# ScalarE's rounding of the next item's scores and of the weights change places in step 6 of a one-core attention kernel

## The chip, the cores and the metric

The kernel runs on one core of a Trainium2 chip (trn2). The metric is the device time of one execution in microseconds (us). Engines are named as the profile names them: PE (TensorE), ACT (ScalarE), DVE (VectorE), POOL (GpSimd), SP (the queue that issues most of the DMAs).

## What is computed

An audio tower: a token mixer (an attention over a spectrum, a feed-forward part, a second attention whose output sets the weights of a moving window), a retention layer, and then a product-key attention layer, which takes most of the time:

```python
q = (x @ Wq).reshape(b, n, HEADS, DIM) * DIM ** (-0.5)
kv_scores, indices = _pk(x, Wq_pk, pk_keys)        # top 16 of 64 x 64 key pairs, softmax over them
k = jnp.einsum('bnhk,bnhkd->bnhd', kv_scores, keys_table[ind])
v = jnp.einsum('bnhk,bnhkd->bnhd', kv_scores, values_table[ind])
sim = jnp.einsum('bihd,bjhd->bhij', q, k)          # causal
out = jnp.einsum('bhij,bjhd->bhid', softmax(sim), v)
```

There are 8 heads, 8 sequences of 344 tokens, and tables of 4096 rows of 64 values and 64 keys for each head.

## The kernel before, in words

Nothing is gathered. For each pair of head and sequence (an item; 64 in all, in the order of the heads) the kernel makes the weight of every one of the 4096 table rows for each of the 344 tokens, zero for all rows but the 16 chosen, and multiplies the table by them on PE. The table has 32 chunks of 128 rows, and an item takes 16 steps (`d` from 0 to 15) of two chunks each:

- **Logarithms of the weights.** `log_weights` (line 981): two fp16 matmuls of a 0/1 matrix `sel` with `X`, 128x344 each, into one of two pairs of PSUM banks (`d % 2`).
- **Weights.** ACT takes the exponential, `exponentials` (line 1218), into `W` in a ring of eight. DVE sets to zero what is below the threshold, `weights` (line 1575), and with that also sets free the PSUM banks.
- **Sum over the table.** `table_sum` on PE. Even steps: fp32 matmuls (line 990). Odd steps (`SPLITS`): `W` is split in a rounded part and the rest, `weights_high` on ACT (line 1223) and `weights_low` on POOL (line 1409), and four matmuls of line 998 and two of line 1002 take the place of the two.

PE runs ahead with the logarithms: in step `d` it first waits for `weights` of `d + 3` (`w_done`), then makes the logarithms of `d + 5`, then the table sum of `d`. ACT in step `d` takes the exponential of `d + 5` and rounds the weights of `d + 3`. Where `d + 5` reaches 16 these belong to the next item. So from step 11 on PE needs the next item's `X`.

`X` of the next item comes by this chain. DVE finds the largest scores; POOL subtracts the thresholds and clamps (`centre_first`, `clamp_scores`, lines 1351, 1356 and 1358, in step 4) into `aS`. In step 6 ACT rounds `aS` to fp16, `high_part` (line 1213, writes `spl`); POOL makes the remainder, `low_part` (line 1403); SP then issues six transposing DMAs from `spl` to `X` (`turn_scores`, line 860), three for the even part and three for the odd part, one behind the other. PE waits for the even part ahead of its step 11 (`x_even`) and for the odd part in step 15 (`x_odd`).

Every engine's order is written out by hand in a loop body, one for each engine. What touches the change:

```python
def high_part(n):
    act.wait_ge(clamped, n * 2 + 2)
    ...
    A(spl[:, :, :, 0, :], aS[:, :, :, :], ACT.Copy).then_inc(high_ready, 1)
```

Step 6 of the other engines: POOL has `low_part` and then `weights_low` of step 9, and in front of them, from step 4, `clamp_scores` and `weights_low` of step 7; in step 7 it goes on with `chosen_weights` (line 1395). DVE has `weights` of step 10, then (in items of even number, `par == 0`) `copy_second_queries`, then `chosen` (line 1615: three small comparisons), then `weights` of step 11. In items of even number ACT has `copy_queries` (line 1243) behind the exponential of step 6. In step 11 PE's table sum is followed by `turn_probabilities` (line 1076), in step 13 by `attention_output` (line 1084), in step 7 by `attention_scores`.

Of the kernel before, what the change touches and what calls it, by code (L numbers as in the profile page):

```python
# [663 lines left out]
def retention_and_keys(nc, ps, hT, x2T, epst, cst, const, weight, wf, sel, eyeb, causb, wq, wo, tables, out):  # L664
# [14 lines left out]
    with ExitStack() as ctx:  # L679
# [96 lines left out]
        def ahead(s):  # L776
            return AHEAD[s]
# [52 lines left out]
        with nc.Block() as block:  # L830
# [335 lines left out]
            def _(act):  # L1166
# [28 lines left out]
                def copy_similarities(n):  # L1195
                    act.wait_ge(sim_mm, n + 1)
                    if not isinstance(n, int) or n > 0:
                        act.wait_ge(a_ready, n * 2)
                    A(sS[:, 0:2, :, :], ps[:, sim_bank(n), 0:256], ACT.Copy)
                    A(sS[0:88, 2, :, :], ps[0:88, sim_bank(n), 256:384], ACT.Copy).then_inc(sim_ready, 1)  # L1200

                def candidate_weights(n):
                    act.wait_ge(rel_ready, n + 1)
                    A(ecs[:, :, :], ecs[:, :, :], ACT.Exp)
                    act.wait_ge(thr_step, n * 2 + 2)
                    A(small[:, EDT, :], small[:, DT, :], ACT.Exp).then_inc(ecs_ready, 1)

                def high_part(n):
                    act.wait_ge(clamped, n * 2 + 2)
                    if not isinstance(n, int):  # L1210
                        act.wait_ge(x_even, n * 48)
                        act.wait_ge(x_odd, n * 48)
                    A(spl[:, :, :, 0, :], aS[:, :, :, :], ACT.Copy).then_inc(high_ready, 1)  # L1213

                def exponentials(i, d):
                    act.wait_ge(main_done, i * NDC + (d - RING + 1 + ahead(main_done)))
                    act.wait_ge(log_mm, i * NDC + (d + 1))
                    A(W[:, d % RING, :, :], ps[:, 2 * (d % 2):2 * (d % 2) + 2, 0:LOUT], ACT.Exp).then_inc(e_done, 1)  # L1218

                def weights_high(i, d):  # L1220
                    act.wait_ge(main_done, i * NDC + (split_before(d, SPLIT_RING) + 1 + ahead(main_done)))
                    act.wait_ge(w_done, i * NDC + (d + 1))
                    A(W_high[:, split_at(d) % SPLIT_RING, :, :], W[:, d % RING, :, :], ACT.Copy).then_inc(high_done, 1)  # L1223

                def table_high(slot, loads, pair, half):

                    act.wait_ge(s_tab[slot], loads * 48)
                    o, rows = part_of(tab_high, slot, pair, half), rows_of(slot, pair, half)
                    A(o, rows, ACT.Copy).then_inc(tab_high_ready, 1)

                def copy_gains(i):
                    act.wait_ge(gains_mm, i + 1)
                    A(gains[:, :], ps[:, MID1, 0:LOUT], ACT.Copy).then_inc(gains_ready, 1)

                def copy_projected_values(i):
                    act.wait_ge(vw_mm, i + 1)
                    act.wait_ge(nmax_done, i * 3 + 3)
                    A(vw[:, 0:2, :], ps[:, MID0, NT * 128:NT * 128 + 128], ACT.Copy)
                    A(vw[0:88, 2, :], ps[0:88, MID1, LOUT:LOUT + 64], ACT.Copy).then_inc(vw_ready, 1)

                def copy_queries(g):
                    act.wait_ge(q_mm, g + (1 + ahead(q_mm)))
                    A(qT[64:128, 0, :], ps[64:128, 5, 0:LOUT], ACT.Copy, scale=D ** -0.5).then_inc(qT_ready, 1)

                def probabilities(i, pj, t):
                    act.wait_ge(nmax_done, i * 3 + 3)
                    m, (bank, c0) = TT[t][1], score_area(t, pj)
                    A(P[0:m, t, 0:TT[t][0] + m], ps[0:m, bank, c0:c0 + TT[t][0] + m], ACT.Exp, bias=nmax[0:m, t:t + 1],  # L1248
                      accum_out=zz[0:m, t:t + 1]).then_inc(p_done, 1)

                def copy_turned_probabilities(i):
                    act.wait_ge(pt_mm, i + 1)
                    A(PT[:, 0, :], ps[:, MID1, 0:LOUT], ACT.Copy)
                    A(PT[0:88, 2, 0:88], ps[0:88, MID1, LOUT:LOUT + 88], ACT.Copy).then_inc(pt_ready, 1)  # L1254
# [31 lines left out]
                class Body:  # L1286
# [4 lines left out]
                    @staticmethod  # L1291
                    def item(i, slot, par, g, pair):
                        nj = 1 - par
                        for d in range(NDC):
                            if d + LEAD < NDC:
                                exponentials(i, d + LEAD)
                            else:
                                exponentials(i + 1, d + LEAD - NDC)
                            if d == 6 and par == 0:
                                copy_queries(g)  # L1300
                            if (d + LEAD - 2) % NDC in SPLITS:
                                if d + LEAD - 2 < NDC:
                                    weights_high(i, d + LEAD - 2)
                                else:
                                    weights_high(i + 1, d + LEAD - 2 - NDC)
                            if d == 2:
                                copy_gains(i)
                            if d == 5:
                                candidate_weights(i + 1)
                            if d == 6:  # L1310
                                high_part(i + 1)
                            if d == 8:
                                copy_similarities(i + 2)
                            if d == 9:
                                copy_projected_values(i)
                                for t in range(NT):
                                    probabilities(i, nj, t)
                            if d == 12:
                                copy_turned_probabilities(i)
                            if d == 11:  # L1320
                                table_high(1 - slot, i // 16 + (1 + slot), pair, par)
# [481 lines left out]
```

## Time and profile before

| | before |
|---|---|
| median of 3 runs | 1924.92 us (1922.6 to 1926.18) |
| profiled execution, its own time | 1926.57 us |
| its span, first to last instruction | 1924.8 us |
| granted PE clock, mean | 0.987 of full |
| PE busy | 1867.0 us (97%) |
| PE weight loads busy | 1408.0 us (73%) |
| DVE busy | 1608.8 us (84%) |
| ACT busy | 1459.5 us (76%) |
| POOL busy | 1317.6 us (68%) |

The span holds some 220 us of token mixer, retention and set-up, and then the 64 items. Times in the rows are microseconds from the start of the span. An item from 962.1 to 988.5 us has an even number and one from 988.5 to 1014.3 us an odd one; these two stand for all the others. In a timeline a row gives the start, the time taken, the engine, line, operation and names, with a count where rows are merged, and in brackets the idle time ahead of it and what ended it. Rows of PE are matmuls, rows of PEld the weight loads that run ahead of them; `k_` is the prefix of this stage's tiles.

### The profile page before, as it was taken

To read this page: it belongs to the slowest core of one execution; us is meant where nothing else is said; L and a number is where in the kernel's file an instruction comes from. 1 tells how busy PE (TensorE), PEld (TensorE's weight loads), DVE (VectorE), ACT (ScalarE), POOL (GpSimd) and SP (SyncE) were. 2 spreads that over 40 slices of the span, in tenths; PEclk is the share of its full clock that TensorE was granted. 3 is DMA by queue.
4 is the path that set the end of the run, shared out by engine and by line. 5 is a ranking of instruction groups with operands and counts; after the bars stand their busy time and mean duration, and the time that the engine had idled before them with its cause. 6 is when DMAs were issued, how large, how long until landed. Compare 5 with 4: busy or idle time off the path is not lost.

```text
span 1924.8 us, 43767 instructions
## 1 busy us (share of the span) xinstructions
PE 1867.0 (97%) x11488; PEld 1408.0 (73%) x11488; DVE 1608.8 (84%) x4825; ACT 1459.5 (76%) x2969; POOL 1317.6 (68%) x1576
## 2 busy tenths in 40 slices
PE   7997899999999999999999999999999999999997
PEld 5765577777777777777777777777777777777775
DVE  4646788888888888888888888888988888888886
ACT  3853488877878777888887778887887787878885
POOL 1112377777777777777777777777777777777775
PEclk8998899999999999999999999999999999999998
DMA  3001110001000200011000200020001100020001
GB/s 110 2 1 48 58 22 21 21 16 61 20 21 21 63 17 17 21 52 33 21 16 17 63 21 21 21 61 17 19 21 32 54 16 17 18 65 21 21 19 28
DMA packets 118622, 58.00 MB, mean 30 GB/s; under 512 B 110224, under 2 KB 116560, under 8 KB 117261
## 3 DMA queue, kind: packets, MB, share of 16 engines
q1 hardware_dynamic: 115778, 56.75, 11.4%
q10 hardware_dynamic: 2795, 0.70, 0.2%
q8 instruction: 18, 0.29, 0.1%
q14 instruction: 31, 0.25, 0.0%
HBM read 24.55 MB, written 0.70 MB: 13 GB/s over the span
## 4 chain that ended last, share of the span: by engine, by line
POOL 42%; issue 38%; PE 7%; POOLq 2%; DVE 1%; SPq 0%; ACT 0%; DMA 0%; DVEq 0%; ACTq 0%
POOL k_W_low L1409 25%; POOL k_aS L1351 3%; POOL k_cand L1365 2%; POOL k_ecs L1395 2%; POOL k_tab_low L1414 2%; PE ps L990 2%; POOL k_aS L1358 2%; PE ps L981 1%; PE ps L998 1%; POOL k_aS L1356 1%; POOLq L1408 1%; POOL k_small L1380 1%; POOL k_small L1381 1%; POOL k_ecs L1376 1%; POOL k_off L1385 1%
## 5 line engine op out<-in xcount | busy, mean ns | idle before, releaser
L1409 POOL TENSOR_TENSOR k_W_low<-k_W,k_W_high 128x688 fp32r<-128x688 f32 x513 | 851.2, 1659 | 320.9 <-ACT k_W_high L1223 317.6
L1218 ACT ACTIVATE k_W<-ps 128x688 f32<-128x688 f32 x1029 | 770.0, 748 | 339.6 <-PE ps L981 327.2
L1575 DVE SCALAR_TENSOR_TENSOR k_W<-ps,k_W 128x688 f32<-128x688 f32 x1028 | 887.9, 866 | 162.9 <-ACT k_W L1218 152.6
L990 PE MATMUL ps<-k_W,k_tab 128*128 128x344 f32 x2048 | 676.4, 453 | 0.0
L981 PE MATMUL ps<-k_X,sel 128*128 128x344 f16 x2058 | 472.4, 311 | 17.1 <-DMA k_X<-k_spl 9.0
L990 PEld LDWEIGHTS ps<-k_W,k_tab 128*128 128x128 f32 x2048 | 366.2, 190 | 126.9 <-issue 0.2
L1223 ACT ACTIVATE k_W_high<-k_W 128x688 fp32r<-128x688 f32 x513 | 398.0, 776 | 0.8
L998 PE MATMUL ps<-k_W_high,k_tab_high 128*128 128x344 f32 x1024 | 386.2, 380 | 0.0
L981 PEld LDWEIGHTS ps<-k_X,sel 128*128 128x128 f16 x2058 | 164.6, 98 | 237.6 <-issue 77.1
L998 PE MATMUL ps<-k_W_high,k_tab_low 128*128 128x344 f32 x1024 | 323.9, 319 | 0.0
L1002 PE MATMUL ps<-k_W_low,k_tab_high 128*128 128x344 f32 x1024 | 246.6, 322 | 0.0
L998 PEld LDWEIGHTS ps<-k_W_high,k_tab_high 128*128 128x128 f32 x1024 | 193.7, 189 | 24.7
L998 PEld LDWEIGHTS ps<-k_W_high,k_tab_low 128*128 128x128 f32 x1024 | 193.9, 189 | 0.0
L1002 PEld LDWEIGHTS ps<-k_W_low,k_tab_high 128*128 128x128 f32 x1024 | 174.7, 188 | 3.0
L1403 POOL TENSOR_TENSOR k_spl<-k_aS,k_spl 128x480 f16<-128x480 f32 x65 | 72.9, 1122 | 56.5 <-ACT k_spl L1213 56.5
L1615 DVE TENSOR_SCALAR k_rc<-k_cand,k_small 128x100 f32<-128x100 f32 x195 | 102.5, 579 | 0.0
L1035 PE MATMUL ps<-k_kv,k_qT 64*128 64x128 f32 (+2 forms) x390 | 97.3, 383 | 0.0
L1248 ACT ACTIVATE cst<-ps,k_nmax 128x128 f32<-128x128 f32 (+2 forms) x195 | 88.9, 487 | 0.0
L1084 PEld LDWEIGHTS ps<-k_vw,cst 128*128 128x128 f32 (+2 forms) x780 | 83.1, 176 | 1.0 <-ACT cst L1254 1.0
L1084 PE MATMUL ps<-k_vw,cst 128*128 128x64 f32 (+2 forms) x780 | 82.3, 256 | 0.7 <-ACT cst L1254 0.7
L1593 DVE TENSOR_REDUCE k_nmax<-ps 128x1 f32<-128x128 f32 (+2 forms) x195 | 67.4, 401 | 16.0 <-PE ps L1035 16.0
L1536 DVE MATCH_REPLACE8 k_rp<-k_top,k_sS 128x64 f32<-128x64 f32 (+1 forms) x396 | 78.2, 206 | 0.3 <-issue 0.3
(237 smaller groups left out, 2308.9 us busy)
## 6 DMA issues: line engine op xcount, KB each, us to landing
k_tab<-in_tables SPq DMA_DIRECT2D x9, 2048.0 KB, 7.2
k_X<-k_spl SPq DMA_TRANSPOSE x390, 2.3
k_xs<-x2T SPq DMA_DIRECT2D x66, 86.0 KB, 2.0
k_qT<-k_qs SPq DMA_DIRECT2D x33, 86.0 KB, 2.0
cst<-in_consts SPq DMA_DIRECT2D x1, 1024.0 KB, 10.0
wts<-in_weights SPq DMA_DIRECT2D x1, 896.0 KB, 7.6
cst<-in_consts SPq DMA_DIRECT2D x1, 874.5 KB, 6.0
xr<-in_xrows SPq DMA_DIRECT2D x1, 750.0 KB
```

Source lines behind the costliest of these rows:

```text
L981: mm = mm_(ps[:, 2 * (d % 2) + k, 0:LOUT], sel[:, (c // 8) % 2, c % 8, :], X[:, par, c // 8, 0:LOUT], start=True, stop=True)
L990: mm = mm_(sums, tab[:, slot, at + k, :], W[:, d % RING, k, :], start=(d == 0 and k == 0), stop=(d == NDC - 1 and k == 1))
L998: mm_(sums, t[:, slot, at + k, :], W_high[:, q % SPLIT_RING, k, :], start=(d == 0 and k == 0 and t is tab_high), stop=False)
L1002: mm = mm_(sums, tab_high[:, slot, at + k, :], W_low[:, q % SPLIT_RING, k, :], start=False, stop=(d == NDC - 1 and k == 1))
L1035: return mm_(ps[0:m, bank, c0:c0 + t0 + m], qT[64:128, pj, t0:t0 + m], kv[64:128, 0:t0 + m], start=False, stop=(t > 0))
L1084: mm = mm_(ps[0:m, MID1, 64 * t:64 * t + 64], PT[0:kn, kt, t0 - k0:t0 - k0 + m], vw[0:kn, kt, :], start=(kt == 0), stop=(kt == t))
L1218: A(W[:, d % RING, :, :], ps[:, 2 * (d % 2):2 * (d % 2) + 2, 0:LOUT], ACT.Exp).then_inc(e_done, 1)
L1223: A(W_high[:, split_at(d) % SPLIT_RING, :, :], W[:, d % RING, :, :], ACT.Copy).then_inc(high_done, 1)
L1248: A(P[0:m, t, 0:TT[t][0] + m], ps[0:m, bank, c0:c0 + TT[t][0] + m], ACT.Exp, bias=nmax[0:m, t:t + 1], accum_out=zz[0:m, t:t + 1]).then_inc ...
L1409: G.tensor_tensor(W_low[:, q % SPLIT_RING, :, :], W[:, d % RING, :, :], W_high[:, q % SPLIT_RING, :, :].bitcast(F32), ALU.subtract).then_i ...
L1575: V.scalar_tensor_tensor(W[:, d % RING, :, :], ps[:, 2 * (d % 2):2 * (d % 2) + 2, 0:LOUT], 0.0, W[:, d % RING, :, :], ALU.is_ge, ALU.mult) ...
L1615: o = V.tensor_scalar(rc[:, t, :], cand[:, t, :], small[:, MX, t:t + 1], None, ALU.is_ge)
```

## The change

In ACT's loop body the call of `high_part` in step 6 moves from behind `weights_high` to in front of it. In an item of even number `copy_queries` stays ahead of both. Nothing is added or removed, and no other engine's order changes.

```diff
@@ -1298,6 +1298,8 @@
                                 exponentials(i + 1, d + LEAD - NDC)
                             if d == 6 and par == 0:
                                 copy_queries(g)
+                            if d == 6:
+                                high_part(i + 1)
                             if (d + LEAD - 2) % NDC in SPLITS:
                                 if d + LEAD - 2 < NDC:
                                     weights_high(i, d + LEAD - 2)
@@ -1307,8 +1309,6 @@
                                 copy_gains(i)
                             if d == 5:
                                 candidate_weights(i + 1)
-                            if d == 6:
-                                high_part(i + 1)
                             if d == 8:
                                 copy_similarities(i + 2)
                             if d == 9:
```

## Rows read from the trace of the kernel before

**Rows 1.** Waits, the whole span: us in total, times, longest.
```profile
PEld ps L981 <- DMA k_X<-k_spl: 43.7, 64, 1.7
```

**Rows 2.** Timeline of PE, steps 10 to 13 of an even item.
```profile
981.10 0.47 PE L981 MATMUL ps<-k_X,sel 128*128 128x344 f16 x2
...
982.97 0.47 PE L981 MATMUL ps<-k_X,sel 128*128 128x344 f16 x2 [0.24 <-DMA k_X<-k_spl]
...
984.78 0.46 PE L981 MATMUL ps<-k_X,sel 128*128 128x344 f16 x2
...
986.23 0.46 PE L981 MATMUL ps<-k_X,sel 128*128 128x344 f16 x2
```

**Rows 3.** Timeline of ACT and POOL, step 6 of the even item.
```profile
975.52 0.78 ACT L1223 ACTIVATE k_W_high<-k_W 128x688 fp32r<-128x688 f32 x1
976.21 0.59 ACT L1213 ACTIVATE k_spl<-k_aS 128x480 f16<-128x480 f32 x1
...
978.97 0.74 ACT L1218 ACTIVATE k_W<-ps 128x688 f32<-128x688 f32 x1 [1.41 <-PE ps L981]
...
976.87 1.10 POOL L1403 TENSOR_TENSOR k_spl<-k_aS,k_spl 128x480 f16<-128x480 f32 x1 [1.46 <-ACT k_spl L1213]
```

**Rows 4.** Timeline of SP, the even item.
```profile
978.07 7.60 SPq L860 DMA_TRANSPOSE k_X<-k_spl  x6
```

**Rows 5.** Timeline of DVE, weights of steps 14, 15 and 16, even item.
```profile
981.74 0.85 DVE L1575 SCALAR_TENSOR_TENSOR k_W<-ps,k_W 128x688 f32<-128x688 f32 x1
...
983.70 0.87 DVE L1575 SCALAR_TENSOR_TENSOR k_W<-ps,k_W 128x688 f32<-128x688 f32 x1
...
985.16 0.84 DVE L1575 SCALAR_TENSOR_TENSOR k_W<-ps,k_W 128x688 f32<-128x688 f32 x1
```

**Rows 6.** Timeline of PE's weight loads, step 13 of the even item.
```profile
986.05 0.10 PEld L981 LDWEIGHTS ps<-k_X,sel 128*128 128x128 f16 x1 [0.20 <-DVE k_W L1575]
```

**Rows 7.** Timeline of PE, steps 10 to 12 of an odd item.
```profile
1006.94 0.47 PE L981 MATMUL ps<-k_X,sel 128*128 128x344 f16 x2
...
1008.57 0.46 PE L981 MATMUL ps<-k_X,sel 128*128 128x344 f16 x2
...
1010.48 0.47 PE L981 MATMUL ps<-k_X,sel 128*128 128x344 f16 x2
```

**Rows 8.** Timeline of DVE, weights of step 15, odd item.
```profile
1009.55 0.88 DVE L1575 SCALAR_TENSOR_TENSOR k_W<-ps,k_W 128x688 f32<-128x688 f32 x1
```

**Rows 9.** Timeline of ACT and POOL, step 6 of the odd item.
```profile
1000.80 0.77 ACT L1223 ACTIVATE k_W_high<-k_W 128x688 fp32r<-128x688 f32 x1
1001.47 0.59 ACT L1213 ACTIVATE k_spl<-k_aS 128x480 f16<-128x480 f32 x1
...
1000.23 1.66 POOL L1409 TENSOR_TENSOR k_W_low<-k_W,k_W_high 128x688 fp32r<-128x688 f32 x1
1002.14 1.14 POOL L1403 TENSOR_TENSOR k_spl<-k_aS,k_spl 128x480 f16<-128x480 f32 x1 [0.25 <-ACT k_spl L1213]
```

**Rows 10.** Timeline of DVE, step 6 of the odd item.
```profile
1000.48 1.47 DVE L1615 TENSOR_SCALAR k_rc<-k_cand,k_small 128x100 f32<-128x100 f32 x1
...
1001.88 0.44 DVE L1615 TENSOR_SCALAR k_rc<-k_cand,k_small 128x100 f32<-128x100 f32 x2
...
1002.24 0.86 DVE L1575 SCALAR_TENSOR_TENSOR k_W<-ps,k_W 128x688 f32<-128x688 f32 x1
```

**Rows 11.** Timeline of PE's weight loads, step 8 of the odd item.
```profile
1004.25 0.11 PEld L981 LDWEIGHTS ps<-k_X,sel 128*128 128x128 f16 x2 [0.15 <-issue]
```

**Rows 12.** Timeline of POOL and DVE in the token mixer.
```profile
67.05 1.24 POOL L220 TENSOR_TENSOR oT<-oz,rz 32x94 f32<-32x94 f32 x1
...
67.15 0.93 DVE L556 TENSOR_TENSOR qz<-qT,heads 128x756 f32<-128x756 f32 x1
```

**Rows 13.** Timeline of POOL and DVE ahead of the items: remainders of the table.
```profile
189.19 1.69 POOL L1414 TENSOR_TENSOR k_tab_low<-k_tab,k_tab_high 128x256 fp32r<-128x256 f32 x2 [1.74 <-ACT k_tab_high L1229]
...
189.26 1.03 DVE L1497 TENSOR_TENSOR k_tab<-k_W 128x344 f32<-128x344 f32 x1
```

## The prediction

> **What bounds the kernel now.** I first read the busy shares: PE is at 97%, so an item costs what PE's order costs, and a gain can only be a moment in which PE stands. The list of waits names one that ends on this chain: PE's weight load for the next item's logarithms waits for `X` once in each of 64 items, 43.7 us in all or 0.68 us each [rows 1]. Weight loads run ahead of matmuls, so less than that is lost. The timeline of PE says how much. From step 12 to step 13 the logarithms' matmuls follow each other after 1.45 us; from step 10 to step 11, the same work, it is 1.87 us in an even item and 1.63 us in an odd one [rows 2, 7]. PE is thus late by 0.42 us and 0.18 us. All items repeat this pattern.
>
> Then I asked what PE would run into next if `X` were there. Before each step's logarithms PE waits for DVE's weights of three steps on. In the odd item the weights of step 15 end at 1009.55 + 0.88 = 1010.43, and PE's step 12 starts at 1010.48 [rows 7, 8]: PE is already held by DVE there, 0.05 us behind it. In the even item step 13's weight load starts at 986.05, again 0.05 us behind the end of DVE's weights of step 16, 985.16 + 0.84 = 986.00 [rows 5, 6]. So DVE stands right behind `X` as the next limit.
>
> **The change, part by part.**
>
> *The rounding of the scores starts earlier.* In the even item it starts at 976.21, one rounding of weights behind 975.52: 0.69 us earlier after the change [rows 3]. POOL had been idle for 1.46 us before `low_part`, so this starts 0.69 us earlier too, at 976.18, and SP's transposes at 977.38 for 978.07 [rows 3, 4]. In the odd item the rounding moves from 1001.47 to 1000.80, 0.67 us, but POOL is busy with `weights_low` of step 7 until 1000.23 + 1.66 = 1001.89; its idle time was 0.25 us, and that is all `low_part` can gain [rows 9]. The clamp that `high_part` waits for is ahead of that `weights_low` in POOL's order, so it was over by about 1000.25, half a microsecond before 1000.80: no new wait.
>
> *What that gives PE, even items.* 0.69 us is more than the 0.42 us by which step 11 is late. But step 11 also wants the weights of step 14, which end at 981.74 + 0.85 = 982.59; with 0.05 us it can start at 982.64, not at 982.55: 0.33 us earlier. Step 12 wants the weights of step 15: 983.70 + 0.87 = 984.57, so a start at 984.62 for 984.78: 0.16 us remain. Step 13 follows 1.46 us later, at 986.08 for 986.23, and its weight load, held at 986.05, just allows it [rows 2, 5, 6]. From step 13 on nothing of DVE's is late; ACT's exponential of step 17 and the copy that `attention_output` waits for follow PE's step 12 and come forward with it. So 0.15 us stays for each even item. The bounds are 0 (DVE takes it all) and 0.42 us (DVE's chain moves too). I take 0.15 because DVE runs without a break from step 14's weights to step 16's, in work that does not hang on step 11.
>
> *Odd items.* Step 11 may start up to 0.18 us earlier, but step 12 is held by DVE at 1010.48 as before [rows 7, 8]. Worth 0, at most 0.18.
>
> *The rounding of the weights is later,* by the 0.5 us or so that `high_part` takes ahead of it. POOL wants it behind `low_part`, which takes 1.10 us from 976.18 on, until 977.28, when the rounding has been over since about 976.8. PE wants it in step 9, some 3 us on. Cost 0. Without that cover, at most 0.59 us an item.
>
> *ACT as a whole* does the same two instructions, and the exponential behind them keeps its place within a tenth; ACT then idles 1.41 us for PE before the next one [rows 3]. Cost 0. *SP:* six transposes, 7.60 us in a row [rows 4], all earlier; the odd part is wanted only in step 15, and the loads queued behind them come earlier or at the same time. Cost 0.
>
> *DVE against POOL, odd items.* This is the unknown. The first of `chosen`'s three comparisons starts at 1000.48 and takes 1.47 us, while the other two take 0.44 us together; it ends at 1001.95, just behind `weights_low` of step 7, at 1001.89 [rows 9, 10]. The two engines exclude each other there. Before the change POOL's next instruction comes at 1002.14, when the comparisons are all but through. After it, `low_part` stands directly behind `weights_low`, at about 1001.87, within hundredths of the second comparison, 1001.88. Who wins? Two places help. Ahead of the items POOL ran two table remainders back to back, and a waiting DVE instruction was still let in between them: it started at 189.26 and was over at 190.29, well before POOL's pair, at 190.88 [rows 13]. And in the token mixer POOL's row starts at 67.05 and DVE's at 67.15, yet DVE ended first, at 68.08, and POOL at 68.29 [rows 12]: POOL's claim comes at least 0.10 us after its row starts. So `low_part` claims at 1001.95 or later, behind the second comparison, and at worst the third waits for it. Then: `low_part` from 1002.0 to 1003.10, third comparison over at 1003.17, weights of step 11 from 1003.09 to 1003.95, PE free to go at 1004.00. PE's step 8 starts its load at 1004.25 [rows 11]: hidden, with 0.25 us left. At best the third is not held either. I take 0 for both.
>
> Sum: 32 x 0.15 = 4.8 us. Against the profiled execution's own 1926.57 us that gives 1921.8; it lies 1.65 us above the median, 1924.92, so the median comes to 1920.1.
>
> **The page.** The Trainium skill, "SBUF — State Buffer", section "Who interferes with whom", says that such a pair of engines shares a port, that whoever issues first has it for the whole instruction, and that issue order decides who blocks. Taken with the starts that rows give, this would make `low_part` the winner over the second comparison, which is the slow rival below. That the later start wins in the token mixer [rows 12] speaks against applying it to POOL's rows by hundredths.
>
> **The rivals.**
>
> *The comparisons are blocked twice (slower).* Place: step 6 of odd items. `low_part` gets in ahead of the second comparison (until 1002.95), `weights_low` of step 9 ahead of the third (until 1004.61, at 1.66 us). The third ends at 1004.68, the weights of step 11 at 1005.46, and PE's step 8 loads at 1005.51 for 1004.25: 1.26 us late. 32 x 1.26 = 40 us, less the 5 gained: 1960. It decides once the weights of step 11 end later than 1004.20. For it: the near tie at 1001.87. Against it: the later start won in the token mixer [rows 12]. The page's rule names the same outcome.
>
> *Nothing that can be measured.* DVE takes the rest as well, or half of it: its weights of steps 15 and 16 need only be 0.15 us later than I have them, by the shift of the comparisons or by ACT. For it: 0.16 and 0.15 us are small beside what an ordering changes elsewhere. 1924 to 1925.
>
> *The whole wait goes.* If DVE's chain comes forward with PE, 32 x (0.42 + 0.18) = 19 us: 1905.7. Against it: odd items are held by DVE now, without any help from `X`.
>
> *The change doesn't do what it says:* `high_part` in its new place waits for the clamp. It would have to end 0.5 us later than it does [rows 9]. I give it no chance of its own.
>
> **How the numbers follow.** Forecast 1920.1 (0.56), its own range 1918 to 1922; nothing measurable 1924.5 (0.24); blocked twice 1960 (0.11); the whole wait 1906 (0.06); the rest, 0.03, a mild loss of some 10 us, if the single block costs a few tenths more than its cover. 0.2% is 3.8 us, about what a measurement of this kernel can tell from no change. The forecast, 4.8, lies just beyond that: I give three quarters of its 0.56 to faster, with the whole wait's 0.06: 0.48. Same: 0.14 + 0.24 = 0.38. Slower: 0.14. The range takes the forecast and the case of nothing, 1915 to 1927, which leaves out 0.2.
>
> **What would show it.** In the changed kernel's timeline `high_part` stands ahead of `weights_high` in each step 6; `low_part` follows it at once in even items and follows `weights_low` without a gap in odd ones. PE's waits for `X` fall from 43.7 us to a few, and its waits for DVE's weights rise. Step 10 to 11 takes about 1.54 us in even items; steps 12 start 0.05 us behind DVE in both parities; even items last 0.15 us less, odd ones the same. A third comparison of some 1.1 us in odd items would be the single block. Wrong I would be if a second comparison lasts over 1 us there, if odd items get longer, or if even items shorten by 0.4.

## The result and the profile after

The changed kernel took 1957.97 us (median, 1956.28 to 1959.81), the kernel before 1924.38 us beside it: a ratio of 1.0173 (1.016 to 1.0186). It is 34 us slower. Forecast were 1920.1 us; the slow rival of the prediction had 1960.

The page's busy shares and the list of waits of the changed kernel:

```profile
PE 1872.4 (96%) x11488; PEld 1405.6 (72%) x11488; DVE 1673.5 (85%) x4825; ACT 1457.3 (74%) x2969; POOL 1316.1 (67%) x1576
```
```profile
PEld ps L981 <- DVE k_W L1575: 76.2, 103, 2.2
PE ps L981 <- DVE k_W L1575: 44.2, 39, 1.6
PEld ps L981 <- DMA k_X<-k_spl: 17.5, 32, 0.9
```

DVE is busy for 64.7 us more (1673.5 for 1608.8) with the same 4825 instructions. What the list puts down to `X` has fallen from 43.7 us, 64 times [rows 1], to 17.5 us, 32 times (whose waits these really are is said further down), and PE now waits for DVE's weights instead (before, its weight loads 28.5 us and its matmuls 8.1).

**Even items** went as forecast. The logarithms' matmuls of PE, steps 10 to 13:

```profile
995.35 0.47 PE L981 MATMUL ps<-k_X,sel 128*128 128x344 f16 x2
996.97 0.46 PE L981 MATMUL ps<-k_X,sel 128*128 128x344 f16 x2
998.88 0.47 PE L981 MATMUL ps<-k_X,sel 128*128 128x344 f16 x2
1000.34 0.46 PE L981 MATMUL ps<-k_X,sel 128*128 128x344 f16 x2
```

From step 10 to step 11 it is 1.62 us for 1.87 [rows 2], and from step 10 to step 13 4.99 us for 5.13. An even item lasts 26.32 us (median) for 26.47 before: 0.15 us less.

**Odd items** last 26.92 us for 25.73, 1.19 us more. Step 6 of an odd item, on ACT, POOL and DVE:

```profile
1014.92 0.59 ACT L1213 ACTIVATE k_spl<-k_aS 128x480 f16<-128x480 f32 x1
1015.42 0.77 ACT L1223 ACTIVATE k_W_high<-k_W 128x688 fp32r<-128x688 f32 x1
...
1014.35 1.66 POOL L1409 TENSOR_TENSOR k_W_low<-k_W,k_W_high 128x688 fp32r<-128x688 f32 x1
1015.97 1.11 POOL L1403 TENSOR_TENSOR k_spl<-k_aS,k_spl 128x480 f16<-128x480 f32 x1
1017.02 1.65 POOL L1409 TENSOR_TENSOR k_W_low<-k_W,k_W_high 128x688 fp32r<-128x688 f32 x1
...
1014.61 1.48 DVE L1615 TENSOR_SCALAR k_rc<-k_cand,k_small 128x100 f32<-128x100 f32 x1
1016.01 1.14 DVE L1615 TENSOR_SCALAR k_rc<-k_cand,k_small 128x100 f32<-128x100 f32 x1
1017.07 1.67 DVE L1615 TENSOR_SCALAR k_rc<-k_cand,k_small 128x100 f32<-128x100 f32 x1
1018.66 0.86 DVE L1575 SCALAR_TENSOR_TENSOR k_W<-ps,k_W 128x688 f32<-128x688 f32 x1
```

POOL now runs three instructions without a gap, and each of DVE's three comparisons waits for one of them: the first ends 0.08 us behind `weights_low` of step 7, the second 0.07 us behind `low_part`, the third 0.07 us behind `weights_low` of step 9. Before, the second and third together took 0.44 us [rows 10]. All 32 odd items show the same: `low_part`'s row starts 0.03 to 0.05 us ahead of the second comparison's, that one takes 1.13 or 1.14 us and the third 1.67 or 1.68. The weights of step 11 end at 1019.52, and PE's step 8 has to wait for them:

```profile
1019.57 0.11 PEld L981 LDWEIGHTS ps<-k_X,sel 128*128 128x128 f16 x2 [1.35 <-DVE k_W L1575]
```

The sum closes: there are 32 items of each kind, 32 x (1.19 - 0.15) = 33 us, measured 34.

### The profile page after: what moved, and what is told of

Read it like the earlier page. It is cut to its first block, busy times and chain, and to the rows that moved or that the text cites. A ratio compares the mean times of both kernels' runs of the same rounds, so it can differ in the third digit from the quotient of the medians.

```text
span 1958.0 us, 43767 instructions
## 1 busy us (share of the span) xinstructions
PE 1872.4 (96%) x11488; PEld 1405.6 (72%) x11488; DVE 1673.5 (85%) x4825; ACT 1457.3 (74%) x2969; POOL 1316.1 (67%) x1576
## 4 chain that ended last, share of the span: by engine, by line
PE 61%; issue 11%; DVE 8%; POOL 6%; ACT 5%; POOLq 0%; DMA 0%; ACTq 0%; SPq 0%; DVEq 0%
PE ps L990 21%; PE ps L981 12%; PE ps L998 11%; PE ps L1002 6%; DVE k_rc L1615 4%; POOL k_W_low L1409 3%; PE ps L1084 3%; DVE k_W L1575 3%; ACT k_W L1218 2%; ACT k_W_high L1223 2%; PE ps L1076 2%; PE ps L1035 1%; PE ps L1012 1%; PE ps L1039 1%; PE ps L1018 1%
## 5 line engine op out<-in xcount | busy, mean ns | idle before, releaser
L1615 DVE TENSOR_SCALAR k_rc<-k_cand,k_small 128x100 f32<-128x100 f32 x195 | 176.3, 956 | 0.0
```

Source lines behind the costliest of these rows:

```text
L1615: o = V.tensor_scalar(rc[:, t, :], cand[:, t, :], small[:, MX, t:t + 1], None, ALU.is_ge)
```

## The experiments

Each run is given beside runs of the kernel before on the same chip; those had medians of 1925.16, 1925.58, 1925.95 and 1926.16 us. Two theories stood at the start. The port theory: in odd items POOL's remainder of the scores gets in between DVE's comparisons. The order theory: what costs is ACT's new order itself, by which the weights of step 9 are rounded later.

**The early rounding in even items only.** Also the half of the change that pays, run by itself.

```diff
-                            if d == 6:
+                            if d == 6 and par == 0:
                                 high_part(i + 1)
...
                             if d == 5:
                                 candidate_weights(i + 1)
+                            if d == 6 and par == 1:
+                                high_part(i + 1)
```

> The scores are rounded first in items of even number only; odd items keep the old order. Port theory (in odd items POOL's remainder of the scores, now directly behind another POOL instruction, gets in between DVE's comparisons): even items 26.32 us as in the changed kernel, odd items 25.73 us as before, so 4.5 us (32 x 0.14) below the kernel before: about 1920. Rival, the order theory (the rounding of the weights of step 9 comes too late, and its remainder on POOL with it): even items should carry a part of the loss, and the time lies above 1930.

Measured: 1919.83 us, ratio 0.9973 (0.9962 to 0.9983). Even items 26.32, odd ones 25.69 us. As the port theory has it.

**The early rounding in odd items only** (the same diff with the parities exchanged).

> The scores are rounded first in items of odd number only. Port theory: even items 26.46 us as before, odd items 26.93 us as in the changed kernel, 32 x 1.20 = 38 us above the kernel before: about 1963. Order theory: the loss is shared between the two kinds of item, so below 1950.

Measured: 1963.78 us, ratio 1.020 (1.0185 to 1.0216); even items 26.46, odd ones 26.89 us. All of the loss lies in the odd items.

**POOL waits for the comparisons.** ACT keeps the changed order.

```diff
                             if d == 6:
+                                pool.wait_ge(z_step, (i + 1) * 2 + 1)
                                 low_part(i + 1)
```

> The changed kernel, but POOL's remainder of the scores also waits until DVE's three comparisons are over. ACT's new order stays whole. Port theory: the second and third comparisons take 0.26 us again, odd items 25.73 us, even items 26.32 us, about 1920. Order theory: nothing of ACT's order is undone and POOL starts later still, so it stays at 1958 or more.

Measured: 1920.26 us, ratio 0.9977 (0.9968 to 0.9986); even items 26.31, odd ones 25.70 us. POOL and DVE in an odd item:

```profile
1000.44 1.10 POOL L1403 TENSOR_TENSOR k_spl<-k_aS,k_spl 128x480 f16<-128x480 f32 x1 [0.51 <-DVE k_rc L1616]
...
998.53 1.47 DVE L1616 TENSOR_SCALAR k_rc<-k_cand,k_small 128x100 f32<-128x100 f32 x1
999.92 0.26 DVE L1616 TENSOR_SCALAR k_rc<-k_cand,k_small 128x100 f32<-128x100 f32 x1
1000.10 0.26 DVE L1616 TENSOR_SCALAR k_rc<-k_cand,k_small 128x100 f32<-128x100 f32 x1
```

POOL stands idle for half a microsecond, and the kernel is 38 us faster than the changed one. ACT's order is untouched, so the order theory is out: the rounding of the weights, later by some 0.5 us, costs nothing.

**One comparison instead of three.**

```diff
-                    for t in range(NT):
-                        o = V.tensor_scalar(rc[:, t, :], cand[:, t, :], small[:, MX, t:t + 1], None, ALU.is_ge)
-                    o.then_inc(z_step, 1)
+                    V.tensor_tensor(rc[:, :, :], cand[:, :, :], small[:, MX, :, None].to_broadcast([128, NT, NCAND]),
+                                    ALU.is_ge).then_inc(z_step, 1)
```

> The changed kernel with the three comparisons in one tensor-tensor instruction of 300 elements against the broadcast threshold. Port theory, one wait for each DVE instruction that needs the port: it waits only for POOL's remainder of the weights of step 7 and takes about 0.2 to 0.3 us more of the port; POOL's remainder of the scores comes behind it by about as much. Odd items 25.73 us, about 1920. If the wait grows with what DVE has to move and not with the number of instructions, or if the order theory holds, it stays near 1958.

Measured: 1919.43 us, ratio 0.9971 (0.9959 to 0.9983); odd items 25.69 us. The single instruction takes 1.72 us in an odd item, the three in the kernel before 1.84 from first start to last end; `low_part` behind it takes 1.33 us for 1.10. Three waits have become one. The edit also changes the kind of instruction (`tensor_tensor` for `tensor_scalar`), so by itself it doesn't show that the number alone matters; the longer `low_part` shows that the new kind still excludes POOL.

**One comparison in the kernel before.**

> The kernel before with the three comparisons in one instruction and the old order on ACT. Nothing of DVE's comparisons was on the path there, so the time is that of the kernel before, 1925, within 0.1%. If it comes to 1920, the gain of the kernel with both was not the earlier rounding of the scores.

Measured: 1925.23 us beside 1925.58, ratio 0.9998 (0.9989 to 1.0007). So the 5 us of the run above are the earlier rounding's.

**The remainder of the scores in two instructions** (a third, then two thirds of it, on POOL).

```diff
-                    G.tensor_tensor(spl[:, :, :, 1, :], aS[:, :, :, :],
-                                    spl[:, :, :, 0, :], ALU.subtract).then_inc(low_step, 1)
+                    G.tensor_tensor(spl[:, 0, :, 1, :], aS[:, 0, :, :], spl[:, 0, :, 0, :], ALU.subtract)
+                    G.tensor_tensor(spl[:, 1:NT, :, 1, :], aS[:, 1:NT, :, :], spl[:, 1:NT, :, 0, :],
+                                    ALU.subtract).then_inc(low_step, 1)
```

> The changed kernel with POOL's remainder of the scores in two instructions, of one third and two thirds. If the engines take turns, one instruction each, the second comparison waits for the first part (about 0.45 us) and the third for the second part (about 0.8 us), and POOL's 1.66 us remainder of the weights comes behind all three: the weights of step 11 end some 1.1 us later than before the change, inside PE's cover of 1.15 us. Odd items 25.7 to 25.9 us, 1920 to 1926. If the wait is for all that POOL has queued, it stays near 1958.

Measured: 1920.84 us, ratio 0.9976 (0.9966 to 0.9986); odd items 25.72 us. POOL and DVE:

```profile
1000.00 0.50 POOL L1403 TENSOR_TENSOR k_spl<-k_aS,k_spl 128x160 f16<-128x160 f32 x1
1000.45 0.80 POOL L1404 TENSOR_TENSOR k_spl<-k_aS,k_spl 128x320 f16<-128x320 f32 x1
1001.20 1.65 POOL L1410 TENSOR_TENSOR k_W_low<-k_W,k_W_high 128x688 fp32r<-128x688 f32 x1
...
1000.05 0.53 DVE L1616 TENSOR_SCALAR k_rc<-k_cand,k_small 128x100 f32<-128x100 f32 x1
1000.49 0.83 DVE L1616 TENSOR_SCALAR k_rc<-k_cand,k_small 128x100 f32<-128x100 f32 x1
1001.24 0.86 DVE L1576 SCALAR_TENSOR_TENSOR k_W<-ps,k_W 128x688 f32<-128x688 f32 x1
```

Here the engines take turns, one instruction each: there are still three comparisons and three waits. The same work on POOL, cut in two, costs nothing, since the 1.65 us piece now stands behind the last comparison, and a delay of 0.83 us for the weights of step 11 fits under PE's cover.

**A short memset ahead of the remainder,** first of one column, then of 128. Both ask when POOL's instruction overtakes the second comparison. The diff is the first's; the second has `pad[:, :]` of 128 columns.

```diff
                             if d == 6:
+                                G.memset(pad[:, 0:1], 0.0)
                                 low_part(i + 1)
```

> The changed kernel with a one-column memset on POOL ahead of its remainder of the scores. Port theory with the order of arrival: the memset may slip in between DVE's first and second comparison but is short; the second comparison then gets the port ahead of the remainder of the scores, and only the third waits for it (about 1.1 to 1.3 us), which the prediction's single-block case calls hidden. Odd items near 25.7 to 25.8 us, about 1920. Rival: whatever POOL queues directly behind is served before DVE's next comparison, however many: the memset makes one more turn and the comparisons still lose two long turns or the second only: if the second still takes 1.1 us and the third 1.67 us, 1958.

Measured: 1959.92 us, ratio 1.0177 (1.0161 to 1.0193), against the 1920 expected. The memset had moved `low_part` by a mere 0.05 us: its row starts level with the second comparison's, and it still goes first. In all 32 odd items the two starts lie within 0.01 us of each other, sometimes with POOL's the later one, and `low_part` went first in each.

```profile
1017.04 0.10 POOL L1451 MEMSET k_pad<- 128x1 f32 x1
1017.09 1.10 POOL L1404 TENSOR_TENSOR k_spl<-k_aS,k_spl 128x480 f16<-128x480 f32 x1
...
1017.09 1.17 DVE L1617 TENSOR_SCALAR k_rc<-k_cand,k_small 128x100 f32<-128x100 f32 x1
1018.18 1.68 DVE L1617 TENSOR_SCALAR k_rc<-k_cand,k_small 128x100 f32<-128x100 f32 x1
```

So this first memset told nothing of what happens when POOL is later. With 128 columns:

> The changed kernel with a memset of 128 columns on POOL ahead of its remainder of the scores; the one-column memset of the run before had moved that remainder by only 0.05 us, to within 0.01 us of the second comparison. Theory, order of arrival: now the remainder's row starts 0.1 us or more behind the second comparison's, which takes 0.26 us; the third alone waits, 1.1 to 1.3 us. The weights of step 11 end before PE's step 8 wants them: the prediction's single block. Odd items 25.7 us, about 1920. Rival, POOL's queued work goes first whatever its start: second 1.1 us or more, third 1.67 us, 1958 or more.

Measured: 1921.66 us, ratio 0.9981 (0.9971 to 0.999); odd items 25.73 us.

```profile
997.78 0.20 POOL L1451 MEMSET k_pad<- 128x128 f32 x1
997.95 1.11 POOL L1404 TENSOR_TENSOR k_spl<-k_aS,k_spl 128x480 f16<-128x480 f32 x1
999.01 1.65 POOL L1410 TENSOR_TENSOR k_W_low<-k_W,k_W_high 128x688 fp32r<-128x688 f32 x1
```
```profile
998.02 1.10 DVE L1617 TENSOR_SCALAR k_rc<-k_cand,k_small 128x100 f32<-128x100 f32 x1
999.04 0.86 DVE L1577 SCALAR_TENSOR_TENSOR k_W<-ps,k_W 128x688 f32<-128x688 f32 x1
```

The row at 998.02 is the third comparison; the second took 0.27 us. This is the prediction's single block: `low_part` 0.12 us behind the second comparison, the third held for 1.1 us, and the loss gone, since the weights of step 11 end in time. An instruction more on POOL, 0.2 us long, brings back 36 us. The second comparison and `low_part` had been 0.04 us apart.

Two readings of this run are left: the earlier row goes first, or the memset used up POOL's turn. Against the second speaks the one-column memset, behind which `low_part` went first all the same, and a pair of rows in the kernel before, without any memset. There `low_part` starts at 1002.14, 0.08 us behind the third comparison [rows 9], and takes 1.14 us where it takes 1.10 alone:

```profile
1002.06 0.26 DVE L1615 TENSOR_SCALAR k_rc<-k_cand,k_small 128x100 f32<-128x100 f32 x1
```

The comparison keeps its 0.26 us. In all 32 odd items of that kernel POOL's row is 0.06 to 0.09 us behind, and DVE goes first.

**What holds PE next.** With the loss gone, steps 12 and 13 wait for DVE in both kinds of item. First DVE's sum and reciprocal of the next item's gains were moved out of the way, on top of the single comparison.

```diff
                             if d == 10:
                                 halves_drop(i + 2, 0)
-                                softmax_sum(i + 1)
...
                             if d == 12:
                                 copy_turned_probabilities(i, nj)
+                                softmax_sum(i + 1)
```

> The changed kernel with one comparison, and DVE's sum and reciprocal of the next item's gains (0.6 us) moved from step 10, ahead of the weights of step 15, to step 12, behind the copy of the turned probabilities. Theory: after the change DVE's weights of steps 15 and 16 hold PE in both kinds of item; 0.6 us less ahead of them frees step 12. Even items gain 0.10 us more (PE's own pace from step 11 on), odd items 0.18 us: about 9 us below 1920, near 1911. Rival: the next limit stands as close as this one (the weights of step 14, or X), then 1917 to 1920.

Measured: 1920.83 us, ratio 0.9969 (0.9957 to 0.9981): no gain. The rival was right that another limit stands as close, but it is ACT, not one of the two it named. ACT and DVE in an odd item:

```profile
1006.97 0.58 ACT L1248 ACTIVATE cst<-ps,k_nmax 88x344 f32<-88x344 f32 x1
...
1007.49 0.78 ACT L1218 ACTIVATE k_W<-ps 128x688 f32<-128x688 f32 x1
```
```profile
1008.30 0.88 DVE L1575 SCALAR_TENSOR_TENSOR k_W<-ps,k_W 128x688 f32<-128x688 f32 x1 [0.54 <-ACT k_W L1218]
```

The exponential of step 15 starts behind the probabilities and ends at 1008.27, where DVE's weights wait 0.54 us for it. So it went ahead of the third probabilities, once alone and once with DVE's sum moved as well.

```diff
-                            if d + LEAD < NDC:
+                            if d + LEAD < NDC - 1:
                                 exponentials(i, d + LEAD)
-                            else:
+                            elif d + LEAD >= NDC:
                                 exponentials(i + 1, d + LEAD - NDC)
...
                                 for t in range(NT):
+                                    if t == NT - 1:
+                                        exponentials(i, NDC - 1)
                                     probabilities(i, nj, t)
```

> The changed kernel with one comparison, and ACT's exponential of step 15 ahead of the third probabilities instead of behind them; DVE's sum stays in step 10. Theory that DVE and ACT reach the weights of step 15 at nearly the same time: freeing ACT alone leaves DVE's sum in the way, so 1917 to 1921, as with one comparison alone. If ACT alone was the limit, 1911.

Measured: 1917.67 us, ratio 0.9954 (0.994 to 0.9967).

> Both moves together: DVE's sum behind the copy in step 12 and ACT's exponential of step 15 ahead of the third probabilities. The weights of step 15 then end about 0.5 us earlier and PE's step 12 goes at PE's own pace: even items 0.10 us and odd items 0.18 us shorter, 9 us in all, near 1911. Rival: the third probabilities, 0.65 us later, hold PE's turning of them in step 11; then no gain or a loss of up to 0.2 us an item.

Measured: 1913.82 us, ratio 0.9936 (0.9922 to 0.9949): 12 us below the kernel before, the fastest version. Even items 26.22, odd ones 25.61 us. The expectation had 9 us beyond the single comparison and got about 7, by the ratios 0.9971 and 0.9936. The sum and the exponential each hide the other: the first alone brings nothing, both together 7. The second alone has 3 us by the ratios, but its interval overlaps that of the single comparison (0.9959 to 0.9983), and by the items it is 1 us (even 26.29 for 26.31, odd 25.69 for 25.69), so a gain of its own is not shown. Step 12 now follows step 11 at PE's own pace (1.82 us, as behind a late step 11 before [rows 2]):

```profile
1001.52 0.47 PE L981 MATMUL ps<-k_X,sel 128*128 128x344 f16 x2
1003.13 0.46 PE L981 MATMUL ps<-k_X,sel 128*128 128x344 f16 x2
1004.95 0.46 PE L981 MATMUL ps<-k_X,sel 128*128 128x344 f16 x2
1006.40 0.46 PE L981 MATMUL ps<-k_X,sel 128*128 128x344 f16 x2
```

**That version with the old order of the two roundings.**

> The fastest version so far (one comparison, DVE's sum in step 12, ACT's exponential of step 15 ahead of the third probabilities), but with the rounding of the scores back behind the rounding of the weights. Theory: X then holds PE's step 11 of even items again, 0.42 us late, and whatever was freed in step 12 is of no use there: even items 26.46 us; odd items keep 25.61 us. 32 x 0.25 = 8 us above the version with the early rounding, about 1922. If the early rounding no longer matters once steps 12 and 13 are free, 1914.

Measured: 1921.92 us beside 1926.16, ratio 0.9979 (0.997 to 0.9988). Even items 26.46, odd ones 25.61 us. The change under study is thus worth 0.4% in this surrounding, against a loss of 1.7% in its own.

## Why the prediction was wrong

*Even items: right.* 0.15 us forecast, 0.15 measured, by the mechanism named. One term on the way was off: step 11 came 0.13 us behind DVE's weights of step 14, not 0.05, so it gained 0.25 us and not 0.33. In the item shown it started at 996.97, for the same two waits; the step is followed by DVE's hold at step 12, so nothing of this reached the sum. The same 0.13 us lay there in the odd item of the kernel before. There the list of waits had put all 64 waits down to `X` [rows 1], but in odd items `X`'s third transpose, issued some 2.5 us behind the first at 1003.38 and 2.3 us in landing, was in by 1008.3, and DVE's weights of step 14, over at 1008.43, came last. So there was no gain to be had in odd items, which last 25.70 us for 25.73 where POOL waits for the comparisons. The forecast that PE's waits for `X` would fall to a few microseconds looks wrong by the list, which still has 17.5 us, but that is the same mistake of the list: in 31 of the 32 waits `X` had landed 0.42 to 0.47 us before the weight load started, and DVE's weights of step 14 had ended 0.12 or 0.13 us before it. One wait for `X` is left, of 0.88 us.

*Odd items, ACT, SP: right.* No new wait for the clamp, the rounding of the weights hidden, POOL's gain limited by `weights_low` of step 7.

*The step that failed* is in "DVE against POOL, odd items": "POOL's claim comes at least 0.10 us after its row starts. So `low_part` claims at 1001.95 or later, behind the second comparison". I had taken that 0.10 us from one pair of rows of the token mixer [rows 12] and laid it on a tie of 0.04 us elsewhere. The prediction's own rows 13 already spoke against it. Unmerged, POOL's two remainders there are

```profile
189.19 0.73 POOL L1414 TENSOR_TENSOR k_tab_low<-k_tab,k_tab_high 128x256 fp32r<-128x256 f32 x1 [1.74 <-ACT k_tab_high L1229]
...
189.87 1.00 POOL L1414 TENSOR_TENSOR k_tab_low<-k_tab,k_tab_high 128x256 fp32r<-128x256 f32 x1
```

and DVE's addition at 189.26 took 1.03 us, where the same instruction takes 0.52 alone. POOL's row was only 0.07 us ahead, and DVE waited for it: had POOL's claim come 0.10 us after its start, DVE would have gone first. POOL's second remainder then took 1.00 us for the first's 0.73, behind DVE. The runs show that here the claim follows the rows' starts as near as they can be read: `low_part` went first when its row started 0.04 us ahead of the second comparison (changed kernel) and when it started level with it (one-column memset), and second when it started 0.12 us behind (128 columns) or 0.08 us behind the third (kernel before). What followed was right in each part. The single block is hidden, as computed; the double block was priced at 1.26 us an odd item and measured 1.19. Only the choice between the two was wrong, and its chance, 0.11, much too low: a tie of 0.01 us between two rows, by the prediction's own reckoning, should have had near even chances, and the range should have held both ends.

*The page.* The Trainium skill, "SBUF — State Buffer", section "Who interferes with whom", says that issue order decides and that whoever issues first keeps the shared port for the whole instruction. The prediction set this rule aside for the token mixer's rows. The trace agrees with it for the comparisons: in the changed kernel, in the halved remainder and with both memsets, each second or third comparison that started level with a POOL instruction or behind it took until 0.06 to 0.08 us after that instruction's end. The token mixer's rows remain an exception that no run explains.

*The rivals.* "Blocked twice" is what happened, at its place, by its mechanism, with 1960 for 1957.97. "The whole wait goes" and "nothing that can be measured" are both excluded by the even items, which gained 0.15 or 0.16 us in every run that had the early rounding in them and three comparisons.

## What to carry to other kernels

Where DVE and POOL exclude each other, a gap in POOL's queue is what lets a run of short DVE instructions through: each of them can lose one whole POOL instruction (here 1.1 and 1.65 us), and bringing a POOL instruction forward can close the gap. Before moving work that feeds POOL, look at what DVE runs at that moment, count its instructions that need the shared port, and make them one, or make POOL wait for them: either was worth some 38 us here. Where two rows would start within a few hundredths of a microsecond, a forecast can't tell the order, though the chip may then keep to it in every item, as it did in all 32 here. The range must hold both sides. And a list that names one cause for a wait on two things should be set against the times at which both came.

## What was not expected of the hardware

Turns between the engines are taken instruction by instruction, however unequal: comparisons of 0.26 us waited for POOL instructions of 0.50, 0.80, 1.10 and 1.65 us, one each. With the 128-column memset the first comparison took 1.64 us for 1.48, as if part of it had waited for the memset; yet the second one's row started 1.4 us behind the first's, as in the changed kernel, so the memset did not simply go ahead of the first. Whether a memset claims differently was not tried. Why DVE won in the token mixer although POOL's row started 0.10 us earlier [rows 12] stays open too. With the early rounding in even items only it is the same (POOL's row at 67.45 took 1.24 us, DVE's at 67.55 took 0.93). There DVE's instruction reads two SBUF tiles instead of one, and POOL's had a gap of 0.05 us ahead of it, but DVE's addition in rows 13 has two SBUF inputs as well and POOL's remainder an idle 1.74 us ahead of it, and there POOL went first. No run took these apart.
